# A graph attention kernel's fused stage: passes written out and the work of steps reordered

## The reference

```python
score = jnp.einsum('ehd,ehd->eh', Q[dst], K[src]) / np.sqrt(HD)
score = score + jax.nn.relu(efeat @ W1 + b1) @ W2 + b2
m = jax.ops.segment_max(score, dst, num_segments=n)
ex = jnp.exp(score - m[dst])
denom = jax.ops.segment_sum(ex, dst, num_segments=n)
alpha = ex / denom[dst]
out = jax.ops.segment_sum(alpha[:, :, None] * V[src], dst, num_segments=n)
```

## Time and profile before

| | us |
|---|---|
| three runs, median (lowest to highest) | 5547.02 (5539.27 to 5548.26) |
| the profiled execution, its own time | 5540.26 |
| its span, first to last instruction | 5538.5 |
| TensorE busy in the span | 4733.7 |
| VectorE, ScalarE, GpSimd busy | 3289.8, 3295.7, 3290.4 |

### The profile page before, as it was taken

The page is one execution under the profiler, slowest core; times in us unless marked ns, Lnnn a source line. Parts: engine busy times, 40 slices in busy tenths (PEclk is TensorE's granted clock), DMA queues, the critical chain, the costliest instruction groups (busy, mean ns, idle before and its releaser), DMA issues. The chain is left out here.

```text
span 5538.5 us, 101095 instructions
## 1 busy us (share of the span) xinstructions
PE 4733.7 (85%) x20748; PEld 2730.0 (49%) x20749; DVE 3289.8 (59%) x7106; ACT 3295.7 (60%) x7926; POOL 3290.4 (59%) x3364
## 2 busy tenths in 40 slices
PE   8899999999999999999799999877777777767766
PEld 5455555555555555555444444444444444444444
DVE  6488888888888888889833333333333333333334
ACT  3488888888888888888644444333333333333333
POOL 0376766777666667667500000277777777777776
PEclk9999999999999999999999999866666666676676
DMA  4577777777777777778543444333333333333334
GB/s 139 173 238 229 228 224 228 229 234 233 224 229 229 231 226 234 225 221 230 164 158 140 141 141 140 131 106 105 105 106 105 105 106 105 105 105 105 105 105 140
DMA packets 542020, 931.72 MB, mean 168 GB/s; under 512 B 102705, under 2 KB 351631, under 8 KB 541712
## 3 DMA queue, kind: packets, MB, share of 16 engines
q0 software_dynamic: 208384, 648.75, 39.9%
q1 hardware_dynamic: 333328, 280.23, 15.8%
HBM read 795.82 MB, written 132.87 MB: 168 GB/s over the span
## 5 line engine op out<-in xcount | busy, mean ns | idle before, releaser
L1037 POOL DMA_INDIRECT kv_rows<-kv_d,idx x1664 | 1700.3, 1022 | 758.1 <-issue 386.5
L1817 PE MATMUL m_sums<-m_rows,m_oh 128*128 x3328 | 1410.2, 574 | 570.3 <-ACT m_rows L1797 497.5
L1754 POOL DMA_INDIRECT m_rows<-msg_d,m_idx x1568 | 1487.3, 949 | 507.8 <-issue 472.8
L1797 ACT ACTIVATE m_rows<-m_rows,m_norm 128x256 f32<-128x256 f32 x1568 | 710.8, 500 | 1268.1 <-DMA m_rows<-msg_d,m_idx 1268.1
L1817 PEld LDWEIGHTS m_sums<-m_rows,m_oh 128*128 128x128 f32 x3328 | 850.7, 279 | 1129.9 <-issue 1002.0
L1839 DVE TENSOR_TENSOR agg<-agg,m_sums 128x256 f32 x832 | 350.5, 421 | 1302.6 <-PE m_sums L1817 1298.9
L1231 PE MATMUL sums<-kv_rows,onehot 128*128 128x264 f32 x3328 | 949.5, 409 | 29.6 <-issue 11.3
L1231 PEld LDWEIGHTS sums<-kv_rows,onehot 128*128 128x128 f32 x3328 | 575.7, 193 | 441.4 <-issue 329.2
L1188 PE MATMUL p_q<-shelf,pickT 128*128 x4992 | 691.9, 275 | 52.8 <-DVE prod L1283 40.4
L1687 PE MATMUL p_m<-wr,h1T 128*128 128x512 f32 x1568 | 710.8, 596 | 0.0
L1283 DVE TENSOR_TENSOR prod<-p_q,kv_rows 128x512 f32<-128x512 f32 x832 | 568.7, 683 | 121.2 <-issue 84.1
(11 more groups left out here) (194 smaller groups left out, 3901.2 us busy)
## 6 DMA issues: line engine op xcount, KB each, us to landing
msg_d<-msg SPq DMA_DIRECT2D x196, 512.0 KB, 2.9
dsts<-dstrow_d SPq DMA_DIRECT2D x208, 256.0 KB
ef_raw<-in_edge_attr_dram SPq DMA_DIRECT2D x195, 256.0 KB
kv_rows<-kv_d,idx POOLq DMA_INDIRECT x1664, 5.1
m_rows<-msg_d,m_idx POOLq DMA_INDIRECT x1568, 2.7
kv_d<-kvo SPq DMA_DIRECT2D x49, 260.0 KB, 2.1
pens<-pens_d SPq DMA_DIRECT2D x52, 192.5 KB
emlp<-mlp_d SPq DMA_DIRECT2D x52, 128.0 KB
```

Source lines behind the costliest of these rows:

```text
L1037: pool.indirect_dma_start(rows[:, lane, k, a:a + KV], None, kv_d[:, :], bass.IndirectOffsetOnAxis(idx[:, half, c:c + 1], 0)).then_inc(gath ...
L1754: pool.indirect_dma_start(rows[:, u, k, :], None, msg_d[:, :], bass.IndirectOffsetOnAxis(idx[:, u // HALF, c:c + 1], 0)).then_inc(gathered ...
L1797: last = nc.scalar.activation(rows[:, u, k, :], rows[:, u, k, :], ACT.Copy, scale=norm[:, bass.ds(2 * g + k, 1)])
L1817: last = nc.tensor.matmul(sums[u % BANKS][:, 0:D], onehot[:, u % HOTS, k, :], rows[:, bass.ds(slot, 1), k, :].rearrange("p a d -> p (a d)" ...
```

## The change

It does four things, all in `attend`.

1. `passes` writes out all 27 bodies; no engine loops any more.
2. The chunk work is spread over steps 0 to 5 of the next chunk: the two scans in steps 0 and 1 (`forward`, `backward`), `up` in step 2, the chain as `carry` (step 2) and `join` (step 3), `down` and `drop` in step 4, `turn_drop` and `weights` in step 5. Before, these stood in steps 0 to 3. `LATE` rises from R + 3 to R + 5 to match.
3. Each step of TensorE gets one piece of the edge network: `hidden` half 0, `mlp_out` half 0, `hidden` half 1, `mlp_out` half 1 and `turn_ef`, in steps 0 to 3 of a quad. Before, step 1 had two pieces and step 3 none. On ScalarE `take_mlp(m)` and `take_ef(m + 1)` now stand in step 0, and the two `take_hidden` in steps 1 and 3.
4. On SyncE `store_mlp(m)`, in place of `store_mlp(m + 1)`, and `load_chunk` stand behind `load_ef(m + 3)`.

```diff
-LATE = R + 3
+LATE = R + 5
...
         def passes(eng, body):
-            body(0)
-            looped = (CHUNKS - 3) // QUADS
-            with eng.Fori(1, looped) as i:
-                body(i)
-            for i in range(looped, PASSES + 1):
+            for i in range(PASSES + 1):
                 body(i)
...
                         load_idx(c + 1, (v // U + 1) % 2)
+                    if is_quad(m + 3):
+                        load_ef(m + 3)
+                    if is_quad(m):
+                        store_mlp(m)
                     if v % U == U - 1 and is_chunk(c):
                         quads = m + 1 if not isinstance(m, int) else min(m + 1, CHUNKS)
                         load_chunk(c, quads)
-                    if is_quad(m + 3):
-                        load_ef(m + 3)
-                    if is_quad(m + 1):
-                        store_mlp(m + 1)
...
-                    if is_quad(m + 1):
-                        if u % U < 2:
-                            take_hidden(m + 1, u % U)
-                        elif u % U == 2:
-                            take_mlp(m + 1)
-                    if u % U == 3 and is_quad(m + 2):
-                        take_ef(m + 2)
+                    if u % U == 0 and is_quad(m):
+                        take_mlp(m)
+                    if u % U == 0 and is_quad(m + 1):
+                        take_ef(m + 1)
+                    if u % U == 1 and is_quad(m + 1):
+                        take_hidden(m + 1, 0)
+                    if u % U == 3 and is_quad(m + 1):
+                        take_hidden(m + 1, 1)
...
-                    if u % R == 3 and is_chunk(c):
+                    if u % R == 5 and is_chunk(c):
                         weights(c, (u // R - 1) % 2)
...
-                    if is_chunk(c) and u % R < 4:
+                    if is_chunk(c):
                         if u % R == 0:
                             score(c, (u // R - 1) % 2)
-                        elif u % R == 1:
+                        elif u % R == 2:
                             up(c)
-                        elif u % R == 2:
+                        elif u % R == 4:
                             down(c)
-                        else:
+                        elif u % R == 5:
                             turn_drop(c)
                     if is_quad(m + 1):
                         if u % U == 0:
                             hidden(m + 1, 0)
                         elif u % U == 1:
                             mlp_out(m + 1, 0)
+                        elif u % U == 2:
                             hidden(m + 1, 1)
-                        elif u % U == 2:
+                        else:
                             mlp_out(m + 1, 1)
-                    if u % U == 2 and is_quad(m + 2):
+                    if u % U == 3 and is_quad(m + 2):
                         turn_ef(m + 2)
...
-                    if is_chunk(c) and u % R < 3:
+                    if is_chunk(c):
                         if u % R == 0:
-                            scans(c)
+                            forward(c)
                         elif u % R == 1:
-                            chain(c, R * c)
-                        else:
+                            backward(c, R * c)
+                        elif u % R == 2:
+                            carry(c)
+                        elif u % R == 3:
+                            join(c)
+                        elif u % R == 4:
                             drop(c)
```

More of the change, by code:

```diff
@@ L1017, in _ @@
             load_ef(1)
-            store_mlp(0)
             load_ef(2)
@@ L1151, in _ @@
             take_hidden(0, 1)
-            take_mlp(0)
-            take_ef(1)
             passes(act, body)
@@ L1289, in dot, with forward @@
                                         AX.X, ALU.add).then_inc(dots_done, 1)
-            def scans(c):
+            def forward(c):
                 hold(dve, score_done, c + 1, dve_go)
@@ L1296, in scans, with backward, linked, flat @@
                 nc.vector.tensor_tensor_scan(fwd[:, :], pens[:, 0:GE], p_score, -BIG, ALU.add, ALU.max).then_inc(fwd_done, 1)
+            def backward(c, s0):
                 hold(dve, fwd_done, c + 1, dve_go)
                 nc.vector.tensor_tensor_scan(top[:, ::-1], pens[:, 1:GE + 1][:, ::-1], fwd[:, ::-1], -BIG, ALU.add, ALU.max).then_inc(top_done, 1)
+                wait(dve, line_down, c)
+                nc.vector.tensor_scalar(first_node[:, :], t["iota"][0:1, :], t["dst"][0:1, bass.ds(2 * s0, 1)], None,
+                                        ALU.is_equal).then_inc(link, 1)
             LINKS = 9
[L1302 to L1305, removed]
-                    else:
[L1307 to L1311, removed]
+            def linked(c, n, scan=False):
+                if scan:
+                    hold(dve, link, LINKS * c + n, dve_go)
+                else:
+                    dve.wait_ge(link, LINKS * c + n)
+            def flat(x):
+                return x[:, :, :].rearrange("a h r -> a (h r)")
+            def by_head(x):
+                return x.rearrange("a (r h) -> a h r", h=H)
+            def pen(x, w):
+                return line[:, x:x + w].unsqueeze(1).to_broadcast([1, H, w])
+            def carry(c):
                 hold(dve, line_in, 16 * (c + 1), dve_go)
@@ L1315, in chain, with join @@
                 nc.vector.tensor_copy(firstmax[:, :, :], by_head(p_line[:, 0:RH])[:, :, ::-1]).then_inc(link, 1)
-                nc.vector.tensor_scalar(first_node[:, :], t["iota"][0:1, :], t["dst"][0:1, bass.ds(2 * s0, 1)], None,
-                                        ALU.is_equal).then_inc(link, 1)
-                linked(1, True)
+                linked(c, 2, True)
                 nc.vector.tensor_tensor_scan(flat(carried), line[:, 0:H * (R + 1)], flat(lastmax), -BIG, ALU.add, ALU.max).then_inc(link, 1)
-                linked(2, True)
+                linked(c, 3, True)
                 nc.vector.tensor_tensor_scan(flat(onward), line[:, H * (R + 1):H * (2 * R + 1)], flat(firstmax), -BIG, ALU.add, ALU.max).then_inc(link, 1)
-                linked(4)
+            def join(c):
+                linked(c, 4)
                 nc.vector.tensor_tensor(by_head(before[:, :]), carried[:, :, 0:R], pen(PEN_ON, R), ALU.add).then_inc(link, 1)
                 nc.vector.tensor_copy(lastmax[:, :, 0:1], carried[:, :, R:R + 1]).then_inc(link, 1)
-                linked(5)
+                linked(c, 5)
                 nc.vector.tensor_tensor(by_head(after[:, :])[:, :, 0:R - 1], onward[:, :, R - 2::-1], pen(PEN_ON + R, R - 1),
                                         ALU.add).then_inc(link, 1)
-                linked(6)
+                linked(c, 6)
                 nc.vector.tensor_tensor(newmax[:, :], before[:, 0:H], onward[:, :, R - 1], ALU.max).then_inc(link, 1)
-                linked(9)
+                linked(c, 9)
                 nc.vector.tensor_tensor(fall[:, :], before[:, 0:H], newmax[:, :], ALU.subtract).then_inc(line_done, 1)
@@ L1396, in body @@
                         v = u - LATE - 1
-                        if v % LOADS == 0:
-                            behind = load_four(nc, dve, t["block"], s - LATE - 1, 0, BLOCKS - 1)
+                        if u == 0 or v % LOADS == 0:
+                            behind = load_four(nc, dve, t["block"], s - LATE - 1 - v % LOADS, 0, BLOCKS - 1)
                         if v % R == 0:
```

## The result

| | us | against before |
|---|---|---|
| before, median of 4 runs | 5547.64 | |
| the change, median of 4 runs (6692.94 to 6726.84) | 6710.01 | ratio 1.209 [1.206, 1.213] |
| the profiled execution's span | 6714.9 | before 5538.5 |

The account below looks back on a forecast made before the run. TensorE sets the pace, VectorE and ScalarE close behind. Chunks of 73.5 us instead of 48.56 add 1197 us over 48, the first quads about 20, LATE 5, to the profiled 5540.3: 6762, forecast 6770 for the median; range 6330 to 7020.

Parts of the forecast that it names:

- The ring: Turn, load issue, store issue, store landed, take_mlp, take_ef, hidden, next turn: TensorE stands 4.4 us in every quad.
- T: The end of the turn of the next edge attributes; what SyncE does behind its wait can't start earlier.
- the rest of the quad: From hidden to the next turn's end: 9.1 us of work, plus 2.2 for the clock.
- The landing taken from SyncE's wait: Store of the edge network's result: 3.0 us waited at the chunk loads plus 1.14, so 4.14 from its issue.
- the quick-landing rival: The slower pace empties the queues, so the store lands in 2.1 us: 6370 us in all; chance 7%.
- The clock: Each 4.4 us standstill of TensorE brings a fall of the granted clock: 2.2 us per quad, between 1.6 and 2.8.
- The chunk loads: Issued behind SyncE's wait and the store, the shift row lands at T + 8.1, delaying score and hidden: 3.5 us per chunk.
- the 0.8 kept for the chain: Waits of the chunk chain left per chunk, in us (bounds 0 and 2.6), since VectorE catches up while TensorE stands.
- The sum: A chunk is 4 x 17.3 + 3.5 + 0.8 = 73.5 us, 48 chunks add 1197 us; forecast 6770.
- The jumps: Writing out the passes removes the loop jumps, 3.8 us of VectorE each: 48 chunks would gain 99 us.
- The chain over five steps: Chunk work spread over five steps: between 0 and 2.6 us of waits per chunk can go.

Follow-up runs that it names:

- the first three expectations: On the change: store ahead of the edge-attribute load, 6327.6 us; store and chunk loads both ahead of it, 6125.9; a second mlp tile, 6599.5.
- written out and one piece per step, SyncE mended by order: The change with store, `dsts` and chunk loads ahead of the edge-attribute load on SyncE, but chunk work in four steps and LATE at R + 3: 5490.0 us.
- all three, SyncE mended by order: The change with store, `dsts` of the quad after next and chunk loads all ahead of the edge-attribute load on SyncE: 5420.4 us.
- all three, SyncE mended by a second tile: The change with two tiles for the raw edge attributes, so SyncE waits for the turn of a quad earlier, all orders kept: 5414.3 us.

## Why the prediction was right, point by point

*The ring.* Predicted: `hidden` at T + 5.95, the rest of the quad 11.3 with its clock, 17.3 in all. In the timelines after, 132 plain quads (500 to 3700 us) have `hidden` at T + 5.7 on the mean, a rest of 11.3 and 17.0 in all. The landing taken from SyncE's wait, 4.14, is 1515.07 - 1510.94 = 4.13 in the quad shown; the 0.25 us came off the issues, since the store now goes out 0.45 after T, not 0.75. With the DMA engines 53% busy instead of 77% the store takes as long as before; the quick-landing rival fell on that. The Trainium skill's fixed cost of about 2 us (DMA: Bandwidth & Descriptors, section "Latency and other measured facts") is about half of the 4.13 measured here.

*The clock.* 2.2 us per quad was the middle of two falls. The rest of a quad, 9.1 us of work, took 11.3, and TensorE has no idle time in it (0.01 us a quad on the mean), so the 2.2 are slower matmuls and the term holds. The group that follows `hidden` at 1517.14 takes 1.93, and 1.16 at the upper level; the granted clock there is at its lower level:

```profile
1517.50:1520.50 3.00, 3.00 (x14) 1.79 (x16) 1.25 (x3) 3.00 (x9) 0.00 (x0) 0.50 0.14 55
```

That the mean fell on the middle is in part luck: in single quads the rest runs from 10.7 to 12.4, and no row told which of the two falls a quad would have.

*The chunk loads.* Predicted 4.3 us per chunk (3.5 and 0.8), measured 21.9 - 17.0 = 4.9. Two terms were too small. The shift row took 2.95 us to land instead of 2.1, and the score came at T + 9.2 instead of 8.4. And the score was priced at 1.05 us, as at the upper clock; behind 7.65 us of idle time the clock is at 0.50, and from the score at 1536.04 to `hidden` at 1538.02 it took 2.0:

```profile
1536.00:1538.00 2.00, 1.96 (x6) 1.36 (x6) 1.95 (x4) 0.51 (x2) 0.00 (x0) 0.50 0.18 48
```

On the other side the rest of such a quad is 10.8, not 11.3, and the 0.8 kept for the chain was too much: its wait in front of `down` is 0.5 (25.3 us in 50 waits), and it stands ahead of `hidden`, where TensorE would have waited for `efT` anyway.

*The sum.* Three plain quads and one with chunk loads make 72.9 us, where 73.5 were predicted. The mean of the 48 chunks is 72.3, since the last of them took 51.8: two of its quads have no attributes left to turn. The difference, 1.2 us a chunk, makes 58 of the 60 us between forecast and result.

*The jumps.* 99 us were reckoned for them, and the sum holds this by building a chunk from quads without a jump; the run with written-out passes alone gives 5542.1 - 5449.8 = 92.

*Where it was incomplete.* The prediction said that what SyncE does behind the wait can't start before T, and then priced the store and the chunk loads but not `dsts`, which is in the same queue. This did not move the forecast, because by the time ScalarE has waited for the store, `dsts` has landed or nearly so: freeing `dsts` alone gave back 31 us. But it made the first three expectations wrong: by the step "a ring through the store", opening that ring cures the change, and it gives back 382 us of 1290. The incomplete step is the list of what stands behind the wait: store, `dsts`, chunk loads, each with its own consumer.

*The chain over five steps.* The prediction took it for a gain of 0 to 2.6 us per chunk. The runs show that it can also be a loss: 2.2 us a chunk (104 / 48) when the edge pieces stay where they were. One piece per step without the spread is a loss too (5490 against 5450; SyncE's order differs as well between these two). There TensorE idles less than with the passes written out alone, 17.5 of 500 us against 21.1, but its clock is 0.97 instead of 1.00: one wait of 1.5 us per chunk is followed by a fall in most chunks. Only together do the two parts gain, 5420 against 5450.

| kernel | us |
|---|---|
| before | 5542 to 5548 |
| passes written out | 5449.8 |
| written out and five steps | 5554.1 |
| written out and five steps, exponentials first | 5469.1 |
| written out and one piece per step, SyncE mended by order | 5490.0 |
| all three, SyncE mended by order | 5420.4 |
| all three, SyncE mended by a second tile | 5414.3 |
| all three, SyncE as in the change | 6710.0 |

So the change with SyncE mended is worth 2.2 to 2.3%, of which the written-out passes alone give 1.7, and what SyncE issues behind its wait for the turn adds 24% to the mended time. What was not tried: the fall of the clock could not be taken away by itself, so its share, about 2.2 of the 6.3 us that a plain quad grew, stays read from the rows.

## What to carry to other kernels

When an event that a queue waits for moves later, list every issue behind that wait and, for each, who waits for it and how long it takes to land; the one that lands last hides the others, so mending one shows the next. A second tile for the one thing that is waited for did as much here as the best order of issues (5414 and 5420 us). And a step that is spread must be looked at on every engine: a piece that moves into a step whose other piece waits for a partner inherits that wait. Where TensorE's idle time is compared, compare its granted clock as well: the run that idled less was the slower one.

## What the runs showed that was not expected

The losses don't add: freeing `dsts` gave 31 us, the store 382, store and chunk loads 584, all three 1290. And the store moved ahead (6328) beats the second mlp tile (6599) although both open the same ring, because the store in front still holds back what is issued behind it on the same queue (`dsts` lands 6.0 us behind the turn instead of 5.1 in plain quads).
